# A graph network on one core: the edge stage and the first layer as one stage

## The reference, cut to what matters

```python
agg = segment_sum((x @ W0)[src] * edge_weight[:, None], dst)     # first layer
x   = layernorm(x + relu(agg))
ph   = noise * arange(1, 33) * (2 * pi / 16)                     # noise embedding, used in layer 2
cond = silu(concat([sin(ph), cos(ph)]) @ f_w1 + f_b1) @ f_w2 + f_b2
```

## Time and profile before

| | us |
|---|---|
| median of 3 runs | 2424.24 (2418.73 to 2425.98) |
| the profiled execution's own time | 2423.89 |
| its span, first to last instruction | 2422.1 |
| busy: TensorE matmuls, VectorE, ScalarE, GpSimdE | 2113.5, 1607.4, 1021.8, 644.7 |

### The profile page before, as it was taken

The page is one execution under the profiler, slowest core; times in us unless marked ns, Lnnn a source line. Parts: engine busy times, 40 slices in busy tenths (PEclk is TensorE's granted clock), DMA queues, the critical chain, the costliest instruction groups (busy, mean ns, idle before and its releaser), DMA issues. The chain is left out here.

```text
span 2422.1 us, 38711 instructions
## 1 busy us (share of the span) xinstructions
PE 2113.5 (87%) x14446; PEld 1597.9 (66%) x14446; DVE 1607.4 (66%) x3166; ACT 1021.8 (42%) x1498; POOL 644.7 (27%) x472
## 2 busy tenths in 40 slices
PE   6888979998899998799899799999798996888784
PEld 5885537887777887677788677788685554333331
DVE  8995354878564877564778554778555045899964
ACT  1112224666343666343666343666330031244442
POOL 0000025100554100543200543200520000376763
PEclk9999989999899999999999999999899997998886
DMA  1011311889420889421788511778845000000001
GB/s 58 34 45 46 103 36 48 152 142 166 91 67 26 145 143 157 105 60 33 131 146 158 116 42 51 122 144 153 193 95 142 17 14 8 1 0 0 1 0 42
DMA packets 488314, 195.74 MB, mean 81 GB/s; under 512 B 441241, under 2 KB 457625, under 8 KB 488133
## 3 DMA queue, kind: packets, MB, share of 16 engines
q1 hardware_dynamic: 488133, 193.31, 38.8%
HBM read 62.94 MB, written 25.45 MB: 36 GB/s over the span
## 5 line engine op out<-in xcount | busy, mean ns | idle before, releaser
L670 PE MATMUL psum<-turned_probability_parts,values_high 125*128 125x125 bf16 x1600 | 287.3, 224 | 55.8 <-DMA turned_probability_parts<-probability_parts 27.0
L862 DVE CUSTOM_DVE_ANT_0 probabilities<-psum,counts 125x1250 f32<-125x1250 f32 x160 | 233.6, 1460 | 128.7 <-PE psum L672 128.3
L1393 ACT ACTIVATE probabilities<-probabilities,row_peaks 125x1250 f32<-125x1250 f32 x160 | 214.6, 1342 | 178.2 <-DVE row_peaks L866 178.2
L672 PE MATMUL psum<-turned_probability_parts,values_low 125*128 125x125 bf16 x1600 | 286.7, 224 | 0.0
L671 PE MATMUL psum<-turned_probability_parts,values_high 125*128 125x125 bf16 x1600 | 286.6, 224 | 0.0
L1587 DVE SCALAR_TENSOR_TENSOR probability_parts<-probabilities,row_masses,probability_parts 125x1250 bf16<-125x1250 f32 x160 | 246.0, 1538 | 8.9 <-ACT probability_parts L1403 8.3
L1914 POOL TENSOR_TENSOR logs_and_shifts<-logs_by_source,target_shifts_spread 125x1250 f32<-125x1250 f32 x80 | 208.1, 2617 | 128.7 <-ACT target_shifts_spread L2047 69.4
L1403 ACT ACTIVATE probability_parts<-probabilities,row_masses 125x1250 bf16<-125x1250 f32 x160 | 214.2, 1338 | 40.0 <-DVE row_masses L874 34.4
L2153 PE MATMUL psum<-probabilities_turned,values_and_ones 125*65 125x512 f32 (+1 forms) x480 | 199.0, 561 | 21.8 <-ACT probabilities_turned L2064 11.4
L670 PEld LDWEIGHTS psum<-turned_probability_parts,values_high 125*128 125x128 bf16 x1600 | 161.1, 101 | 77.4 <-issue 75.5
L453 ACT ACTIVATE norm_std<-norm_moments,norm_eps 125x1 f32<-125x1 f32 x120 | 35.3, 295 | 331.9 <-DVE norm_moments L449 331.9
(11 more groups left out here) (292 smaller groups left out, 5155.8 us busy)
## 6 DMA issues: line engine op xcount, KB each, us to landing
weight_stage<-in_L_gnn_m_w SPq DMA_DIRECT2D x32, 256.0 KB, 2.6
block_inputs_kept<-nodes SPq DMA_DIRECT2D x8, 896.0 KB
counts_kept<-counts_by_target_rows SPq DMA_DIRECT2D x10, 625.0 KB, 3.6
logs_kept<-counts SPq DMA_DIRECT2D x1, 5468.8 KB
nodes<-block_inputs_kept SPq DMA_DIRECT2D x12, 448.0 KB
turned_probability_parts<-probability_parts SPq DMA_TRANSPOSE x320, 3.6
counts_by_target<-counts_kept SPq DMA_DIRECT2D x2, 2187.5 KB
logs_by_source<-logs_kept SPq DMA_DIRECT2D x1, 4375.0 KB
```

What stands on the lines that cost most here:

```text
L670: pe.matmul(out, lh, rh, start=first, stop=False, skip_group_check=True)
L672: return pe.matmul(out, ll, rh, start=False, stop=last, skip_group_check=True)
L862: dve.tensor_tensor_reduce(prob[0:TILE, T % 2, :], scores, fx.count_src[0:TILE, i, 0:NODES], scale, MASKED, ALU.add, ALU.max, p[:, 0:1]).t ...
L1393: nc.scalar.activation(prob[0:TILE, T % 2, :], prob[0:TILE, T % 2, :], ACT.Exp, bias=fx.peak[0:TILE, T % 2, 1:2], accum_out=fx.mass[0:TILE ...
```

## The change

The two functions become one, `edge_layer`, in one block without the barrier between them. What was the first layer is placed between the bands:

- after band b, from band 4 on, three of four bands have one unit of transposes (4, 4 or 2 of them) in one bank;
- after band b, from band 5 on, stands one edge sum: one group q of 128 targets and one chunk c, ten float32 matmuls of 128 columns. ScalarE copies the four chunks of a group after the fourth sum (`copy_sums`), which is after the bands 8, 12, ..., 36;
- the noise phase is worked out by VectorE in the bands 1 to 7; the two noise products come in three pieces each after the bands 11, 15, 19 and 23, 27, 31;
- the logarithms go by groups of 128 targets over all sources, in place: after band 20, 22, ..., 34 and 39 one group each, on ScalarE (`plain_logs`) and then on VectorE (`log_group`);
- the loads of the noise inputs, biases and W0 are issued during the edge stage, the write of the logarithms to HBM after the last of them;
- the products with W0 follow the last edge sums, the first of them in between, now with six PSUM banks instead of two.

The diff, cut to its core:

```diff
-def edge_bands(nc, fx, psum, src, dst, weight, count_rows, x):
+def edge_layer(nc, fx, psum, src, dst, weight, count_rows, x, log_rows, w0, noise, f_w1, f_b1, f_w2, f_b2, bq, bk, b1):
...
-        def unit(u):
-            return psum[:, (6 + u % 2) * BANK:(7 + u % 2) * BANK]
+        TURN_BANK, SUM_BANK = psum[:, 6 * BANK:7 * BANK], psum[:, 7 * BANK:8 * BANK]
+        SUMS_LAG = SPAN + 1
+        INNER_AT, COND_AT, SINE_AT = {11: 0, 15: 1, 19: 2}, {23: 0, 27: 1, 31: 2}, 9
+        LOGS_AFTER = {20 + 2 * q: q for q in range(GROUPS0 - 2)}
+        LOGS_AFTER[BANDS - 1] = GROUPS0 - 2
+        def turn_at(b):
+            return (b // SPAN - 1, b % SPAN) if b >= SPAN and b % SPAN < 3 and b // SPAN <= GROUPS0 else None
+        def sums_at(b):
+            g = b - SUMS_LAG
+            return (g // CHUNKS, g % CHUNKS) if 0 <= g < GROUPS0 * CHUNKS else None
+        def width(q):
+            return min(128, NODES - 128 * q)
...
+            sp.wait_ge(zeroed, 2)
+            sp.dma_start(phase[:, :], noise.rearrange("n a -> a n").broadcast_to([2 * FREQS, NODES])).then_inc(n_loaded, 16)
+            sp.dma_start(fw1[:, :], f_w1).then_inc(n_loaded, 16)
+            sp.dma_start(fb1[:, :], f_b1.rearrange("(p a) -> p a", a=1)).then_inc(n_loaded, 16)
...
+            for k, v in enumerate((bq, bk, b1)):
+                sp.dma_start(fx.qkb[:, k, :], v.rearrange("i (c p) -> p (i c)", p=128),
+                             allow_slow_non_contiguous=True).then_inc(small, 16)
+            sp.wait_ge(ready, 1)
+            for c in range(CHUNKS):
+                sp.dma_start(w_sb[c][:, :], w0[c * 128:(c + 1) * 128, :]).then_inc(w_loaded, 16)
             for q in range(GROUPS0):
                 sp.wait_ge(unturn, 3 * q + 3)
                 sp.dma_start(count_rows[q * 128:(q + 1) * 128, :], kept[:, q % 2, :]).then_inc(fx.counts_kept[q % 2], 16)
             sp.wait_ge(x_loaded, 16)
+            sp.wait_ge(small, 48)
+            sp.wait_ge(log_ready, GROUPS0)
+            for a, z in ROW_PARTS:
+                sp.dma_start(log_rows.rearrange("(t p) s -> p t s", p=TILE)[a:z], fx.count_src[a:z, :, 0:NODES]).then_inc(fx.logs_kept, 16)
...
+            pool.memset(fw2[:, :], 0.0).then_inc(zeroed, 1)
...
+            def log_group(q):
+                counts = count_src[0:TILE, :, 128 * q:128 * (q + 1)]
+                dve.wait_ge(log_plain, q + 1)
+                step(dve.tensor_scalar(absent[0:TILE], counts, -1.0, MASKED, ALU.is_lt, ALU.mult))
+                dve.scalar_tensor_tensor(counts, counts, HDIM1 ** 0.5, absent[0:TILE], ALU.mult, ALU.add).then_inc(log_ready, 1)
...
                 if b >= 1:
                     weights_of(b - 1)
+                noise_step(b)
+                if b - 1 in COND_AT:
+                    condition_low(COND_AT[b - 1])
+                if b in LOGS_AFTER:
+                    log_group(LOGS_AFTER[b])
                 begin = end
             weights_of(BANDS - 1)
+            log_group(GROUPS0 - 1)
+            for i in range(TILES + 1):
...
+                    if i == 0:
+                        dve.wait_ge(sums, GROUPS0 * CHUNKS)
+                    dve.wait_ge(prod, i + 1)
+                    dve.scalar_tensor_tensor(here, product_bank(i), 0.0, here, ALU.max, ALU.add).then_inc(added, 1)
...
-            def turn_group(q):
-                pe.wait_ge(band_copied, SPAN * (q + 1))
-                for u in range(3):
...
+            def turn_unit(q, u):
+                if u == 0:
+                    pe.wait_ge(band_copied, SPAN * (q + 1))
+                pe.wait_ge(unturn, 3 * q + u)
+                for j in range(4 * u, min(4 * u + 4, TILES)):
+                    mm = pe.transpose(TURN_BANK[:, (j % 4) * TILE:(j % 4 + 1) * TILE], count_src[0:TILE, j, q * 128:(q + 1) * 128],
+                                      ident[0:TILE, 0:TILE])
+                mm.then_inc(turn, 1)
+            def inner_piece(k):
+                a, z = CUTS[k]
+                pe.wait_ge(emb_ready, 2)
+                pe.wait_ge(unturn, 3 * (INNER_BAND[k] // SPAN))
+                pe.matmul(TURN_BANK[0:COND, 0:z - a], fw1[:, :], turns[:, a:z], start=True, stop=True).then_inc(inner_prod, 1)
+            def condition_piece(k):
+                a, z = CUTS[k]
+                pe.wait_ge(inner_ready, 3)
+                pe.wait_ge(unturn, 3 * (COND_BAND[k] // SPAN))
+                pe.matmul(TURN_BANK[0:96, 0:z - a], fw2[:, :], inner[:, a:z], start=True, stop=True).then_inc(cond_prod, 1)
+            def edge_sum(q, c):
+                if c == 0:
+                    pe.wait_ge(summed, min(SPAN * (q + 1), BANDS))
+                    pe.wait_ge(sums_ready, CHUNKS * q)
+                n = width(q)
+                for k in range(TILES):
+                    mm = pe.matmul(SUM_BANK[:, c * 128:c * 128 + n], fx.nodes[0:TILE, k, c * 128:(c + 1) * 128],
+                                   weight_src[0:TILE, k, q * 128:q * 128 + n], start=(k == 0), stop=(k == TILES - 1))
+                mm.then_inc(sums, 1)
+            def first_product(t):
+                pe.wait_ge(sums_ready, CHUNKS * -(-TILE * (t + 1) // 128))
+                if t >= 6:
+                    pe.wait_ge(added, t - 5)
+                for c in range(CHUNKS):
+                    mm = pe.matmul(product_bank(t), sum_t[c][:, t * TILE:(t + 1) * TILE], w_sb[c][:, :], start=(c == 0), stop=(c == CHUNKS - 1))
+                mm.then_inc(prod, 1)
+            def after_band(b):
+                if turn_at(b):
+                    if b - 1 in INNER_AT:
+                        pe.wait_ge(inner_ready, INNER_AT[b - 1] + 1)
+                    if b - 1 in COND_AT:
+                        pe.wait_ge(cond_low, COND_AT[b - 1] + 1)
+                    turn_unit(*turn_at(b))
+                if b in INNER_AT:
+                    inner_piece(INNER_AT[b])
+                if b in COND_AT:
+                    condition_piece(COND_AT[b])
+                if sums_at(b):
+                    edge_sum(*sums_at(b))
...
                 with pe.Fori(begin, end) as n:
                     product(b, n)
-                if b % SPAN == 0 and b > 0:
...
+                after_band(b)
                 begin = end
-            turn_group(GROUPS0 - 1)
+            for b in range(BANDS, BANDS + SUMS_LAG):
+                after_band(b)
+                if b == BANDS:
...
+                    pe.wait_ge(band_copied, BANDS)
+                    pe.wait_ge(summed, BANDS)
+                    first_product(0)
+            for t in range(1, TILES):
+                first_product(t)
...
+            def copy_sums(q):
+                n = width(q)
+                act.wait_ge(sums, CHUNKS * (q + 1))
+                for c in range(CHUNKS):
+                    nc.scalar.activation(sum_t[c][:, q * 128:q * 128 + n], SUM_BANK[:, c * 128:c * 128 + n], ACT.Copy).then_inc(sums_ready, 1)
+            def plain_logs(q):
+                act.wait_ge(turn, 3 * q + 3)
...
+                counts = count_src[0:TILE, :, 128 * q:128 * (q + 1)]
+                nc.scalar.activation(counts, counts, ACT.Ln, bias=fx.tiny[0:TILE, :]).then_inc(log_plain, 1)
+            def after_band(b):
+                if turn_at(b):
+                    copy_unit(*turn_at(b))
+                if sums_at(b) and sums_at(b)[1] == CHUNKS - 1:
+                    copy_sums(sums_at(b)[0])
+                if b == SINE_AT:
+                    act.wait_ge(emb_ready, 1)
...
+                if b in LOGS_AFTER:
+                    plain_logs(LOGS_AFTER[b])
...
                 act.wait_ge(oh_free, SETS * end + SETS)
...
                 nc.scalar.activation(count_src[0:TILE, :, b * BAND:(b + 1) * BAND], view[:, :, 0, :], ACT.Copy).then_inc(band_copied, 1)
-                if b % SPAN == 0 and b > 0:
...
+                after_band(b)
+            for b in range(BANDS, BANDS + SUMS_LAG):
+                after_band(b)
+                if b == BANDS + 2:
+                    plain_logs(GROUPS0 - 1)
...
```

More of the change, by code:

```diff
@@ L94, in edge_bands @@
         count_src, weight_src, ident, ones = fx.count_src, fx.weight_src, fx.ident, fx.ones
+        place = packer(nc, VALUES_AT + 5248)
+        sum_t = [place(f"edge_sums_turned_{c}", [128, NODES], F32) for c in range(CHUNKS - 1)]
+        sum_t.append(packer(nc, HEADW_AT)(f"edge_sums_turned_{CHUNKS - 1}", [128, NODES], F32))
+        place = packer(nc, WORK1)
+        w_sb = [place(f"first_weight_{c}", [128, DIM], F32) for c in range(2)]
+        place = packer(nc, HEADW_AT + 5152)
+        fw1 = place("noise_weight_1", [2 * FREQS, COND], F32)
+        fw2 = place("noise_weight_2", [COND, 96], F32)
+        fb1 = place("noise_bias_1", [COND, 1], F32)
+        fb2 = place("noise_bias_2", [96, 1], F32)
+        lane_i = place("lane_number_int", [2 * FREQS, 1], I32)
+        lane = place("lane_number", [2 * FREQS, 4], F32)
+        w_sb.append(place("first_weight_2", [128, DIM], F32))
+        w_sb.append(packer(nc, CONDS_AT + 5024 + 10016)("first_weight_3", [128, DIM], F32))
```

(38 more changed lines are left out.)

251 lines of the change are left out of this document (70 added, 181 removed).

## The result

The changed kernel takes 2467.1 us (median of 4 runs, 2462.3 to 2469.2), the kernel before, run beside it, 2421.5 (2414.2 to 2426.0). The ratio is 1.0188 [1.0172, 1.0204]: 45.6 us slower, where 26.9 were predicted. The sign, the place and the mechanism of the logarithms were as predicted; the waits of the noise phase were missing.

What follows compares the result with a forecast made beforehand. The prediction took TensorE to bound the merged stage. From 2423.9 us, -22.5 (unhindered path) + 38.0 (logarithm waits) + 11.4 (low clock) = +26.9 gave 2451 us, range 2431 to 2471.

Steps and rivals of the forecast that it cites:

- The bound moves to TensorE: Merged stage: TensorE becomes the bound instead of VectorE; bands with a sum come every 5.6 to 6.1 us.
- The rival of weight loads: Edge sums on TensorE: unhidden weight loads set the pace, 3.9 us a sum, 58 us more, 2509 us; chance 0.04.
- The short sums: Four edge sums of 98 columns on TensorE: 1.75 us each, against 2.28 us for a full sum.
- the row of 0.11 us: Float32 matmul in the last layer, 128 weight columns, 125 moved, 0.11 us start to start; nearest row for the edge sums.
- What an unhindered stage would give: TensorE's path through the merged stage if nothing held it up: end at 318.3 instead of 340.8.
- the -22.5: Merged stage: 22.5 us gained by TensorE's path if nothing held it up.
- The logarithms: VectorE waits for ScalarE's `plain_logs` after bands 20 to 34: four TensorE gaps of 6.2 and four of 3.3, 38.0 us lost.
- The rival that this wait is covered: `log_group` on VectorE: the wait for the logarithms is covered, so the 22.5 us gain stands, 2401 us; chance 0.07.
- The clock: TensorE's clock falls behind the logarithm gaps: 2.1 us per long gap, half of 1.5 per short one, 11.4 us lost.
- The rival of a full clock: TensorE's clock stays full behind the gaps: +15.5 us, 2439 us; chance 0.20.
- the cost of the noise phase: VectorE before band 5: seven small instructions (0.9 us) and four passes of 0.87, 4.4 us in all; band 5 at 48.2.
- Parts that cost nothing: Among others the noise passes of bands 5 to 7 on VectorE, 1.5 to 1.7 us each, covered by VectorE's room.

Runs made afterwards that it cites:

- Experiment 5: The changed kernel with every edge sum made in two halves, of its first 64 columns and the rest, ten float32 matmuls each: 2550.6 us, ratio 1.0543.
- Experiment 6: The changed kernel with ScalarE's logarithms one band earlier, each noise wait ahead of the next step, and the logarithm groups two bands later: 2401.6 us, ratio 0.9929.
- experiment 7: Experiment 6 with the noise phase four bands later, in bands 5 to 11, the noise products later too, and logarithms from band 24 on: 2397.9 us, ratio 0.9923.
- Experiment 1: The changed kernel with ScalarE's logarithms of a group taken one band earlier, VectorE's part left in place: 2419.6 us, ratio 0.9994.
- Experiment 4: The changed kernel with the eight gaps on TensorE filled with 24 or 13 float32 matmuls that nobody reads: 2452.3 us, ratio 1.0136.
- experiment 2: The changed kernel with VectorE's wait for each noise step moved from behind that step to directly ahead of the next one: 2456.7 us, ratio 1.0149.

## Why the prediction was right in kind and short in size

**The bound moves to TensorE: right.** Where nothing waits, band follows band by TensorE's work alone. From its timeline:

```profile
138.24 3.11 PE L453 MATMUL psum<-onehot_band,onehot_source 125*125 x50
141.19 0.60 PE L464 MATMUL psum<-identity,counts 125*128 125x125 f32 x4
141.62 2.40 PE L489 MATMUL psum<-weights,nodes 125*128 125x128 f32 x20
143.95 0.33 PE L445 MATMUL psum<-zero_row 1*125 1x2 bf16 x3
144.21 3.11 PE L453 MATMUL psum<-onehot_band,onehot_source 125*125 x50
```

5.97 us from product to product, inside the 5.6 to 6.1 given. A sum costs 2.33 of it (2.28 taken). The rival of weight loads that set 3.9 us a sum is out. The short sums were a small miss: 1.75 was taken by the column, but they took 2.21 or 2.23 each. The last three, and what follows them:

```profile
345.70 6.84 PE L489 MATMUL psum<-weights,nodes 125*128 125x98 f32 x60
352.38 31.09 PE L499 MATMUL psum<-first_weight,edge_sums_turned 128*125 128x512 f32 x72
```

From start to start that is 6.68/60 = 0.111 us for 98 columns, against 0.117 for 128. Experiment 5 says why the scaling failed; it cost 1.9 us.

The pace measured was 0.115 and 0.117 us with 64 and 128 columns moved. The prediction was right to weigh the sum against the row of 0.11 us and wrong to go on scaling by columns below it.

**What an unhindered stage would give: right within 3 us.** The prediction put its end at 318.3, with the noise passes in the bands 1 to 4. Experiment 6, which has them there, ends at 321.1 with some of their gaps left; experiment 7, which has them out of VectorE's way, at 316.5. From band 5's product on, experiment 7 takes 272.1 us (44.38 to 316.5) where the prediction has 270.1. So the -22.5 was a sound term, though not for this order.

**The logarithms: right.** 38.0 against 40.0: the gaps as read from the program's order, 6.2 and 3.3 foretold, 6.09 and 3.54 found. The copies of the sums were cheaper (0.65 us until the logarithm instead of 1.0), 0.35 us of idle time came ahead of the one-hots (208.99), the table load of 1.3 once. Experiment 1 shows the cause, not only the place. The rival that this wait is covered needed the gaps under 22.5 us together.

**The clock: right in kind, mis-sized.** 11.4 was taken with 2.1 us for a long gap, what the six matmuls of the earlier trace rows lost (4.37 us against 2.31), and with half of the short gaps; all four lowered it. The products took 5.24, 5.08, 5.00 and 5.40 us after the long gaps and 4.66 after the short ones, against 3.11: 8.3 + 6.2 = 14.5. Experiment 4 is in keeping with that: seven of the eight came back, 12.9 us of the 14.5, and its stage ended 13.6 us earlier. Its median time fell by 14.8 us. The product after a short gap and the one after a long gap, in the changed kernel (columns as above):

```profile
190.20:194.70 4.50, 4.50 (x51) 4.43 (x51) 4.50 (x10) 0.00 (x0) 0.00 (x0) 0.62 0.02 5
210.60:215.50 4.90, 4.90 (x51) 4.90 (x52) 4.87 (x11) 0.00 (x0) 0.00 (x0) 0.56 0.00 0
```

Behind the means of 0.62 and 0.56 stands a granted clock of 0.50 for most of each product, from 191.0 to 194.0 and from 210.6 to 214.8. All eight gaps of 3.54 us and more had the low clock behind them, with means of 0.53 to 0.63, and not the half of the short ones that I took. Nor was the clock within a gap a sign: in the changed kernel it was 1.00 within a gap of 3.54 us too (186.5 to 190.1), and low only behind it. (Behind the gap of 2.7 it was 1.00 as well, from 584.2 to 587.2 in the kernel before.) But the clock was low behind gaps of 1.36 to 2.4 us too: 0.50 behind one of 1.36 us in experiment 5, a mean of 0.62 behind the 2.37 us ahead of band 2 of the changed kernel. The rival of a full clock, at 2439, is out.

**The step that failed is the cost of the noise phase.** The prediction counted "seven small instructions" and "four passes of 1,250 columns", said "all 4.4 count", put the first product of band 5 at 48.2, and named the passes of bands 5 to 7 among the "Parts that cost nothing". The product came at 55.14, and band 8's at 77.75, 22.6 later where 17.4 follow from the prediction's terms: 6.9 + 5.2 = 12.1 us missed. I costed the instructions and not the wait that `step` puts behind each. The waits at a band's end left VectorE idle for some 1.85 us each; with them moved (experiment 2), band 8's product came 9.4 us earlier. TensorE had six gaps in a row, ahead of bands 2 to 7, and four of them also lowered the clock (6.2 us of the 12.1). Room in VectorE's busy time doesn't cover this: a band of 4.15 us of work, a pass of 1.45 and 1.85 us bare make 7.45, more than the 5.6 to 6.1 of TensorE.

The sum: 12.1 (noise) + 2.0 (gaps) + 3.1 (clock) + 1.9 (short sums) = 19.1, against 18.8 us by which the stage ended later than the prediction's sum has it (318.3 + 38.0 + 11.4 = 367.7, measured 386.5). That 2467 still lies inside the stated 2431 to 2471 is partly luck: the high end was made of longer gaps, a longer low clock and slower sums, most of which didn't come, and holds nothing for the noise phase, the largest part of the miss.

## What to carry to other kernels

Where two engines run in a hand-written order, a step asked of one engine must be placed at least one iteration before the other waits for it; the same logarithms cost 48 us in the place right after the band and nearly nothing one band earlier, and moving them alone took the loss away; the gain of 0.7 to 0.8% came with the noise waits moved too. But not before its data are ready: group 7, asked for one band too early, cost a gap of 3.76 us. Put a wait in front of the instruction that needs it, not at the end of an iteration: at a band's end it cost VectorE 1.8 us here, between two passes 0.04. And where the trace shows the low clock behind gaps, count a TensorE gap as its length plus what the slow product behind it loses.

## What the runs showed of the hardware that was not expected

- A wait of VectorE for its own last instruction, ahead of a loop's start, costs 1.8 us (20 waits, 36.5 us), shown as idle by "issue" or, wrongly, by a buffer of TensorE. Between two passes the same wait costs 0.04 us.
- Behind gaps of 1.93 and 1.95 us TensorE's clock was low in the early bands (a mean of 0.62), where in the kernel before it was 1.00 in one of 2.7 us and behind it. Nor does the length decide by itself: the gap of 2.3 us ahead of band 5 was followed by a product of 3.10 us in the changed kernel and, with the same code up to there, by one of 4.38 us at a mean of 0.67 in experiment 1. From the first band to band 5 that kernel differs in nothing. In experiment 5 even gaps of 1.36 to 1.39 us were followed by the low clock three times of four (granted clock 0.50 over the product of 5.59 us). Which gaps do it was not settled.
- A float32 matmul instruction with 128 columns of weights takes nearly the same time from start to start whether it moves 64, 98 or 128 columns: 0.115, 0.111 and 0.117 us.
